# Slots of the second expert mixture inverted by one-hot matmuls, rows fetched per block, first eight blocks fixed

## What is computed

```python
d2 = jnp.sum(xs * xs, axis=-1, keepdims=True) + jnp.sum(centroid * centroid, axis=-1)[None, :] - 2.0 * (xs @ centroid.T)
dist = jnp.sqrt(jnp.maximum(d2, 1e-12))
w, sel = jax.lax.top_k(dist, K)
w = jax.nn.softmax(w.astype(jnp.float32), axis=1).astype(x.dtype)
...
for e in range(E):
    h = jax.nn.silu(xs @ Wg[e] + bg[e]) * (xs @ W1[e] + b1[e])
    out = out + we[:, e:e + 1] * (h @ W2[e] + b2[e])
```

## Time and profile before

| | us |
|---|---|
| median of three runs | 869.1 |
| the three runs | 865.69, 869.1, 869.47 |
| the profiled execution, device time | 866.02 |
| its span, first to last instruction | 864.2 |
| PE busy | 740.8 (86%) |
| DVE busy | 558.0 (65%) |
| ACT busy | 414.8 (48%) |
| POOL busy | 266.5 (31%) |

### The profile page before, as it was taken

The page is one execution under the profiler, slowest core; times in us unless marked ns, Lnnn a source line. Parts: engine busy times, 40 slices in busy tenths (PEclk is TensorE's granted clock), DMA queues, the critical chain, the costliest instruction groups (busy, mean ns, idle before and its releaser), DMA issues.

```text
span 864.2 us, 13607 instructions
## 1 busy us (share of the span) xinstructions
PE 740.8 (86%) x4770; PEld 618.3 (72%) x4770; DVE 558.0 (65%) x1030; ACT 414.8 (48%) x886; POOL 266.5 (31%) x232
## 2 busy tenths in 40 slices
PE   6999999998988399989997998888993089999995
PEld 3688888888954278469974676667662089999994
DVE  3469999998459799276665566776344046556651
ACT  4544444442352189354433565666561046655561
POOL 0174544441006244400025012223213514444442
PEclk9999999999999699879999999998885589999998
DMA  7700000000150000000005665530302559999983
GB/s 242 301 2 18 18 18 18 18 1 1 40 238 0 0 2 2 1 0 1 9 1 141 145 163 132 123 87 2 118 1 67 185 190 282 312 317 314 312 246 65
DMA packets 31249, 89.35 MB, mean 103 GB/s; under 512 B 4310, under 2 KB 22038, under 8 KB 27806
## 3 DMA queue, kind: packets, MB, share of 16 engines
q1 hardware_dynamic: 21805, 42.64, 16.5%
q0 software_dynamic: 9376, 45.84, 16.4%
HBM read 77.25 MB, written 13.85 MB: 105 GB/s over the span
## 4 chain that ended last, share of the span: by engine, by line
PE 54%; DVE 13%; issue 5%; DMA 4%; ACT 4%; POOL 2%; POOLq 0%; SPq 0%; DVEq 0%; ACTq 0%
PE PS L449 50%; POOL token_slots L1544 2%; DMA XB<-token_slots 2%; DVE RW L1721 2%; PE PS L987 1%; DVE SM L2019 1%; DVE WK L1781 1%; PE PS L621 1%; DVE WK L1778 1%; DVE RO L1724 1%; DMA KST<-mask_rows 1%; PE PS L838 1%; PE PS L933 1%; DVE M L2028 1%; PE PS L958 1%
## 5 line engine op out<-in xcount | busy, mean ns | idle before, releaser
L1439 POOL TENSOR_TENSOR PRODL<-RW,PRODH 128x361 fp32r<-128x361 f32 x64 | 64.8, 1015 | 113.1 <-ACT PRODH L1097 109.4
L449 PE MATMUL PS<-CTXH,WKV0H 128*128 128x362 f32 x256 | 86.3, 337 | 9.5 <-DVE RW L1677 8.9
L2019 DVE TENSOR_REDUCE SM<-PS 100x1 f32<-100x362 f32 x128 | 64.8, 531 | 43.9 <-PE PS L449 43.1
L449 PE MATMUL PS<-CTXL,WKV0H 128*128 128x362 f32 x256 | 84.6, 330 | 0.0
L449 PE MATMUL PS<-CTXH,WKV0L 128*128 128x362 f32 x256 | 84.2, 329 | 0.0
L1286 ACT ACTIVATE WK<-PS 120x400 f32<-120x400 f32 (+1 forms) x96 | 48.3, 507 | 43.2 <-PE PS L449 42.3
L449 PEld LDWEIGHTS PS<-CTXH,WKV0H 128*128 128x128 f32 x256 | 48.7, 190 | 15.9 <-DVE RW L1677 11.0
L449 PE MATMUL PS<-KST,QST 97*100 97x362 f32 x128 | 53.7, 431 | 6.4 <-DMA KST<-mask_rows 3.6
L1724 DVE TENSOR_REDUCE RO<-RW 128x100 f32<-128x400 f32 x64 | 56.1, 877 | 2.2
L1097 ACT CAST PRODH<-RW 128x361 fp32r<-128x361 f32 x64 | 31.8, 496 | 53.7 <-DVE RW L1677 53.5
L1561 POOL DMA_INDIRECT out<-YO,TROW x20 | 32.0, 1598 | 79.1 <-DVE YO L2146 75.0
(11 more groups left out here) (302 smaller groups left out, 2068.1 us busy)
## 6 DMA issues: line engine op xcount, KB each, us to landing
KST<-keys_by_head SPq DMA_DIRECT2D x24, 362.0 KB
keys_by_head<-KTHL SPq DMA_DIRECT2D x8, 724.0 KB, 3.4
CTX<-ctxT SPq DMA_DIRECT2D x16, 361.0 KB, 6.6
token_slots<-slots SPq DMA_DIRECT2D x1, 2580.0 KB, 19.5
XB<-token_slots SPq DMA_DIRECT2D x20, 129.0 KB
RW<-WGU SPq DMA_DIRECT2D x1, 2304.0 KB, 8.6
RW<-WKV SPq DMA_DIRECT2D x1, 2048.0 KB, 9.9
RB<-W SPq DMA_DIRECT2D x1, 1368.0 KB
```

What stands on the lines that cost most here:

```text
L449: return pe.matmul(out, lhsT, rhs, start=start, stop=stop)
L1439: pool.tensor_tensor(low, raw, high, ALU.subtract).then_inc(sem["a_products_low_ready"], 1)
L2019: dve.tensor_reduce(SM1[:, q % 2, j:j + 1], PS[0:S, i % 2, 0:KVE], AX_X, ALU.max, negate=True).then_inc(sem["c_maximum_found"], 1)
```

## The change

The scatter of rows goes. In its place the kernel works out, for each slot, which token it holds:

- DVE builds, for each of the 16 groups of 100 pairs, a one-hot matrix of the pair's place in its block (POSITION, 100x128) and one of its block (HOME, 100x20), the latter times the token's number (NAMED) and times its weight in two parts (WEIGHED).
- PE multiplies POSITION by NAMED and sums over the 16 groups. The result holds, at partition p and column k, the number of the token in slot p of block k, plus one. DVE turns it into the row to read (XROW, vacant slots read row 0) and the row to add to (TROW). A second set of 16 products gives the slots' weights (WSLOT).
- The normed tokens are stored once as `token_rows` in DRAM, by SP. POOL fetches the 128 rows of a block by an indirect transfer (`gather_rows`), each after the one before has landed. SP's loads of XB and the copy of `slots` go.
- Block k for k below 8 is expert k's first block; blocks 8 to 19 hold what overflows. So the weight rows of the first eight blocks are known without the router. Their weight loads move ahead: block 0's to SP inside the attention stage, blocks 1 and 2 to POOL before its last batch of that stage, block 3 and down weights 1 right after. The casts of block 0's weights move on ACT to quads 26 and 29 of the attention, the subtractions on DVE to before the output projection's additions. `owners()`, the experts of blocks 8 to 19, moves into block 1.
- The copy of the token rows goes from ACT to DVE. The sum of squares goes from PE (16 of 32 products) to ACT, which squares the rows with an accumulator, 8 operations of 100x256. The square root is taken of the two largest distances only, after the choice. Tables of functions are loaded ahead (`preload_act_table_set`).

The diff, cut to its core (a line "..." marks what is left out):

```diff
@@ -424,21 +442,17 @@
+            load(ROUTE, t["route"], "moe1_small_loaded")
+            load(RAW[0], t["W1"][0:P], "moe1_small_loaded")
             sp.wait_ge(sem["c_turned_scores_summed"], 12 * B)
-            load(RAW[0], t["W1"][0:P], "moe1_small_loaded")
+            sp.wait_ge(sem["moe1_small_loaded"], 48)
+            load(BRAW, t["b1g"], "moe1_small_loaded")
             load(DOWN[0], t["W2"][0:P].rearrange("p (t c) -> p t c", t=6), "moe1_small_loaded")
-            load(ROUTE, t["route"], "moe1_small_loaded")
-            load(BRAW, t["b1g"], "moe1_small_loaded")
-            sp.wait_ge(sem["moe_turned_copied"], 10)
+            sp.wait_ge(sem["rows_copied"], 4)
+            sp.dma_start(XROWS.rearrange("(b s) c -> s b c", s=S), ROWS[:, :, :]).then_inc(sem["rows_stored"], 16)
+            sp.wait_ge(sem["moe_turned_copied"], 6)
...
-            sp.wait_ge(sem["rows_scattered"], 16 * 2 * B)
-            for k in range(NBLK):
-                if k:
-                    sp.wait_ge(sem["tokens_loaded"], 16 * k)
-                if k >= 4:
-                    sp.wait_ge(sem["rows_out_ready"], 2 * (k - 3))
-                load(XB[:, k % 4, :], XSC[k * P:(k + 1) * P], "tokens_loaded")
...
@@ -935,20 +949,24 @@
             for b in range(B):
-                pe.wait_ge(sem["router_squares_ready"], 3 + b // HB)
-                pairs = [(XC[:, k, tok(b)], CENT2[:, k, :]) for k in range(KD)]
-                pairs += [(SQ[:, k, tok(b)], ONES[:, 0:8]) for k in range(KD)]
-                for c, (lhsT, rhs) in enumerate(pairs):
-                    m = mm(PS[0:S, 6, b * 8:(b + 1) * 8], lhsT, rhs, c == 0, c == len(pairs) - 1)
+                for k in range(KD):
+                    m = mm(PS[0:S, 6, b * 8:(b + 1) * 8], XC[:, k, tok(b)], CENT2[:, k, :], k == 0, k == KD - 1)
+            m.then_inc(sem["router_scores_summed"], 1)
+            pe.wait_ge(sem["router_result_ready"], 4)
+            mm(PS[:, 5, 0:B * 8], TRI[:, S:S + P], RTH[:, :], True, True).then_inc(sem["router_scores_summed"], 1)
+            mm(PS[0:S, 7, 0:B * 8], TRI[:, 0:S], RTH[:, :], True, False)
+            for b in range(1, B):
+                m = mm(PS[0:S, 7, 8 * b:B * 8], TRI[:, S:2 * S], RTH[:, 0:8 * (B - b)], False, b == B - 1)
             m.then_inc(sem["router_scores_summed"], 1)
             rows_of(X, 6)
-            chosen = RT[:, 6, :]
-            pe.wait_ge(sem["router_result_ready"], 3)
-            pe.wait_ge(sem["moe1_small_loaded"], 80)
-            mm(PS[0:S, 7, 0:B * 8], EARLIER, chosen, True, False)
-            for b in range(1, B):
-                mm(PS[0:S, 7, 8 * b:B * 8], ONES[0:S, 0:S], chosen[:, 0:8 * (B - b)], False, b == B - 1)
-            mm(PS[:, 5, 0:B * 8], AVG[0:S, :], chosen, True, True).then_inc(sem["router_scores_summed"], 1)
+            for i in range(2 * B):
+                pe.wait_ge(sem["slot_rows_ready"], 2 + i // B)
+                m = mm(PS[:, 7, 64:64 + NBLK], POSITION[:, i, :], NAMED[:, i, :], i == 0, i == 2 * B - 1)
+            m.then_inc(sem["router_scores_summed"], 1)
+            pe.wait_ge(sem["router_result_ready"], 7)
+            for i in range(2 * B):
+                m = mm(PS[:, 7, 96:96 + 2 * NBLK], POSITION[:, i, :], WEIGHED[:, i, :, :], i == 0, i == 2 * B - 1)
...
+                if q in (26, 29):
+                    gu_high(0, (q - 26) // 3)
...
+            act.preload_act_table_set("sqrt_and_others")
+            for i in range(4):
+                act.wait_ge(sem["rows_copied"], i + 1)
+                for x in range(2):
+                    act.activation(SQUARES[:, 2 * i + x, :], ROWS[:, 2 * i + x, :], ACT.Square,
+                                   accum_out=RTC[:, 7, 2 * i + x:2 * i + x + 1]).then_inc(sem["router_squares_ready"], 1)
...
-            copy_rows(ROWS[:, 0, :, :], 2)
             act.wait_ge(sem["moe1_small_loaded"], 80)
             act.wait_ge(sem["zeros_set"], 7)
             act.copy(BROWS[0:40, 0:2 * HID1], BRAW).then_inc(sem["bias_rows_ready"], 1)
-            act.wait_ge(sem["zeros_set"], 8)
-            gu_high(0, 0)
-            gu_high(0, 1)
+            gu_high(1, 0)
             act.wait_ge(sem["router_scores_shifted"], 2)
-            act.activation(RT[:, 0, :], RT[:, 0, :], ACT.Sqrt).then_inc(sem["router_function_taken"], 1)
-            copy_rows(RESID, 6)
+            act.activation(FAR, pairs(TOPS), ACT.Sqrt).then_inc(sem["router_function_taken"], 1)
+            act.preload_act_table_set("exp_and_others")
             act.wait_ge(sem["router_scores_shifted"], 3)
             act.activation(RTC[:, 2, :], RTC[:, 2, :], ACT.Exp).then_inc(sem["router_function_taken"], 1)
+            act.preload_act_table_set("silu_and_others")
+            for i in range(4):
+                act.wait_ge(sem["moe_turned"], 6 + i + 1)
+                act.copy(RESID[:, 2 * i:2 * i + 2, :],
+                         PS[0:S, i, :].rearrange("p (x c) -> p x c", x=2)).then_inc(sem["moe_turned_copied"], 1)
+            gu_high(1, 1)
...
+                if b == B - 2:
+                    pool.wait_ge(sem["router_result_ready"], 3)
+                    pool.wait_ge(sem["c_turned_scores_summed"], 12 * (B - 1))
+                    gather_weights(1)
+                    gather_weights(2)
...
-            pool.wait_ge(sem["slots_cleared"], 16)
-            for c in range(2):
-                pool.wait_ge(sem["router_result_ready"], 4 + c)
-                for b in range(B):
-                    pool.indirect_dma_start(XSC, bass.IndirectOffsetOnAxis(ap=SLOT[:, c, b:b + 1], axis=0),
-                                            ROWS[:, c, b, :], None).then_inc(sem["rows_scattered"], 16)
...
+            def gather_rows(k):
+                if k:
+                    pool.wait_ge(sem["tokens_loaded"], 16 * k)
+                if k >= 4:
+                    pool.wait_ge(sem["moe_turned"], 10 + k - 3)
+                pool.indirect_dma_start(XB[:, k % 4, :], None, XROWS,
+                                        bass.IndirectOffsetOnAxis(ap=XROW[:, k:k + 1],
+                                                                  axis=0)).then_inc(sem["tokens_loaded"], 16)
...
+            pool.wait_ge(sem["expert_weights_low_ready"], N0 + 2)
+            gather_weights(3)
+            gather_down(1)
+            pool.wait_ge(sem["rows_stored"], 16)
+            pool.wait_ge(sem["router_result_ready"], 5)
+            gather_rows(0)
+            gather_rows(1)
             pool.wait_ge(sem["router_result_ready"], 6)
-            gather_weights(1)
             pool.wait_ge(sem["out_stored"], 16)
-            gather_weights(2)
-            gather_down(1)
             for k in range(NBLK + 1):
-                if k + 3 < NBLK:
+                if k + 3 == E1:
+                    pool.wait_ge(sem["router_result_ready"], 9)
+                if k and k + 3 < NBLK:
                     pool.wait_ge(sem["expert_weights_low_ready"], N0 + 2 * k + 2)
                     gather_weights(k + 3)
+                if k + 2 < NBLK:
+                    gather_rows(k + 2)
...
+            gu_low(0, 0)
+            gu_low(0, 1)
...
+            for i in range(4):
+                dve.wait_ge(sem["moe_turned"], 2 + i + 1)
+                dve.tensor_copy(ROWS[:, 2 * i:2 * i + 2, :],
+                                PS[0:S, i, :].rearrange("p (x c) -> p x c", x=2)).then_inc(sem["rows_copied"], 1)
...
+                dve.wait_ge(sem["router_squares_ready"], 10)
+                link(dve.tensor_tensor(v(6), wide(RTC[:, 7, :]), CSQ.unsqueeze(1).to_broadcast([S, B, 8]), ALU.add))
...
+                link(dve.tensor_tensor(v(4), before, over(FIRST), ALU.add))
+                link(dve.scalar_tensor_tensor(v(3), before, float(P), over(OFFSET), ALU.is_ge, ALU.mult))
+                link(dve.tensor_tensor(v(3), v(3), v(4), ALU.add))
+                both = RT[:, 1:3, :].rearrange("p c (b e) -> p c b e", b=B)
+                mine = RT[:, 4:6, :].rearrange("p c (b e) -> p c b e", b=B)
+                link(dve.tensor_tensor(mine, both, v(3).unsqueeze(1).to_broadcast([S, 2, B, E1]), ALU.mult))
+                link(dve.tensor_reduce(SLOTS, mine, AX_X, ALU.add))
+                link(dve.tensor_scalar(OPENS, SLOTS, 0.5 - P / 2, GRID, ALU.add, ALU.add))
+                dve.scalar_tensor_tensor(SLOTS, OPENS, -GRID, SLOTS, ALU.add, ALU.subtract)
+                along = lambda a, n: a.unsqueeze(2).to_broadcast([S, 2 * B, n])
+                link(dve.tensor_tensor(HOME, STARTS[0:S].unsqueeze(1).to_broadcast([S, 2 * B, NBLK]),
+                                       along(pairs(OPENS), NBLK), ALU.is_equal))
+                dve.tensor_tensor(NAMED[:, :, :].rearrange("p (c b) k -> p c b k", c=2),
+                                  HOME.rearrange("p (c b) k -> p c b k", c=2),
+                                  TOKEN.unsqueeze(1).unsqueeze(3).to_broadcast([S, 2, B, NBLK]),
+                                  ALU.mult).then_inc(sem["slot_rows_ready"], 1)
                 for c in range(2):
```

(32 more changed lines are left out.)

223 lines of the change are left out of this document (125 added, 98 removed).

## The result

The changed kernel takes 873.57 us, the median of 20 runs (868.09 to 879.93), against 868.97 for the kernel before, the median of 20 as well. The ratio is 1.0057 with a 95% interval of 1.0037 to 1.0077: **0.6% slower**, where the prediction said 3% faster. The profiled execution took 873.65 us with a span of 871.8, 7.6 us longer than the span in the earlier trace rows. The medians are 4.6 us apart: 3 of the 7.6 are there because the execution in the earlier trace rows was a quick one.

The account below looks back on a forecast made before the run. Taking PE to bound the blocks and a serial POOL queue plus load the hole before them, it summed 26.0 + 1.0 - 0.5 = 26.5 us: 866.0 to 839.5, adjusted toward the median to 841.0 us; range 835.5 to 850.

Parts of the forecast that it names:

- What bounds the kernel: Opening step: PE bounds the blocks at 7.86 us each; the hole before them is POOL's scatters, then a load.
- Part 1: Norm's end to the router's first step: start at 649.2 us against 649.82 before, 0.6 us earlier.
- Part 2: Router's first step to the slot lists: index ready at 661.7 us, second 16 products lying beside the gather.
- Part 3: Fetching the rows: hand-over 0.3 us, landing 3.2, tokens there at 665.2 instead of 691.26, 26.0 us gained.
- Part 4: First blocks: block 1 follows block 0 after 8.0 us, 1.0 us gained; owners' steps lose 0.5.
- Part 5: Edits costed at nothing: weight casts, subtractions and POOL's early gathers in the attention stage, POOL's row-fetch issue in the blocks.
- Rival (b): Blocks: row fetches become a serial loop, block at least landing plus 0.3 us; 888 us at 10.2 landing; chance 0.05.
- (a): Head stays longer through a slower first gather, products, hand-overs, block 0 and owners: 9.0 us lost, 850; chance 0.15 with (c).
- (c): Early weight fetches land late or upset the attention stage; first load costs 5.0 us, casts 2.7: 848.7; counted with (a).
- (d): More gained in head and first blocks, squares included (1.8 us): 3.9 us better, 837.1; chance 0.04.
- the sum: Whole kernel: 26.0 + 1.0 - 0.5 = 26.5 us gained, giving 839.5, or 841.0 us adjusted toward the median.

Follow-up runs that it names:

- all four edits: Changed kernel with rows fetched three blocks ahead and before W1, early weight fetches after the attention stage, DVE's subtractions behind the row copies: 841.51 us, ratio 0.9685.

## Why the prediction was wrong

**What bounds the kernel** was read rightly for the kernel before: with a fetch that comes in time PE sets 7.86 us a block again.

**Part 1** put the router's first step 9.3 us behind the norm's end. It took 6.8 (644.58 to 651.37): the squares follow each other every 0.40 us with their accumulator reads beside them (1.8 us less), and the bias subtraction took 1.57 us, not 2.14. But the norm ended at 644.58, not 639.89, so the step stood at 651.37.

**Part 2** gave 12.5 us to the index; it took 12.2 (651.37 to 663.57). The products behind the second POSITION, the last 8 of 16, were in it with 1.2 us (662.15 to 663.39), as forecast.

**Part 3** gave 3.5 us from the index to the tokens. Fetch 1 follows the landing of fetch 0 and starts at 667.64, which puts that landing near 667.4, 3.8 us after the index: 0.8 for the hand-over (0.3 forecast), 3.1 for the landing (3.2 forecast). PE was still in the slot weights' products until 668.15. Part 2 had these "beside the gather"; they cost about 0.8 us. The net gain up to block 0's turn was 23.1 us of the 26.0.

**Part 4** said 1.0 us gained in the first blocks less 0.5 for the owners: 1.9 gained up to turn 3.

**Part 5 is the step that failed**, in two of its sentences. The first and larger is "In the blocks DVE loses a cast and POOL gains an issue of about 1 us against 3.52 busy of 7.86". It priced the fetch by POOL's busy time. The cost of an operation on an in-order queue that waits is its place: the fetch of block j+4 stands behind the output add of block j, W2 and W1, and has 15.7 us less 6.6 and 4.5 to land, 4.6 us. Block 4's took 8.1. That cost 32.4 us in 16 intervals. Three ahead, or the same two ahead from an earlier place, gave them back; one ahead cost 183 us more. The landing itself was in reach of the prediction: the earlier trace rows has a down gather at 4.9 to 10.2 us, median 6.7.

The second is that POOL's early fetches, "two times 1.3 us", stand before operations "wanted only for the second half of that projection", with DVE's subtractions beside them at no cost. The fetches alone cost nothing (19.8 us from projection to norm); the subtractions stretched whatever POOL had beside them, a product from 1.03 to 3.90 us (21.0) or, together with the fetches, an issue from 0.95 to 4.06. That is 2.4 of the 4.2 us more between projection and norm; the rest is PE at a lower clock, and what lowered it stays open.

**Rival (b)** had the right sign and the right place (PE waiting for rows in the turns), for the wrong reason. It took the block to be the landing plus 0.3 us, deciding the sign from 9.0 on. At 8.1 that gives 8.4 us; the measured 9.88 comes from a cycle over two blocks with the output add in it. Without the serial wait nothing changed. That SP's queue would have kept its turn did not matter either: in a queue of its own the load still took 8.1 us. So its 5% stood mainly for a wait that costs nothing, and a lead that is too short had no rival of its own. Its remark that each fetch stands right behind 1.4 MB of weights did hold, with at least 1.5 us of landing.

**Rivals (a) and (c)** were paid for in part, the 4.2 us of the attention stage, though not through the load or ACT's casts that (c) named. (a) also adds 1.4 us for block 0 where Part 4's own bound, 9.6 against 8.0, gives 1.6. **(d)** had the squares right.

Apart from those two sentences the sum holds: with three blocks ahead and the fetches moved the kernel takes 840.24 us, where 841.0 was forecast for the change as made. That it comes so near is partly luck. In that trace block 0's turn comes 25.9 us earlier than before, of 26.0 forecast, because 2.5 us won ahead of the router and 0.3 behind it make up for 1.9 in the attention stage and 1.1 between index and turn; the first blocks give 2.1 us where 0.5 was the net. That version, at 0.9679 of the kernel before, is the best found; the one with all four edits (0.9685) cannot be told from it.

## What to carry to other kernels

When a load moves from one queue to another, write down what stands ahead of it there, what that waits for, and how many tiles later the load is wanted; the time from the last such wait to the deadline, less the issues in between, must exceed the landing under traffic. An issue slot of 1 us says nothing about it. And DVE operations like these subtractions, long and with both inputs in SBUF, want a place where POOL has nothing urgent, issuing an indirect transfer included.

## What the runs showed of the hardware that I had not expected

**POOL is held up beside a DVE subtraction of two SBUF tiles.** Its product took 3.40 to 3.90 us instead of 1.03, and issues of indirect transfers are stretched just so. In the blocks of the changed kernel, POOL and DVE:

```profile
751.56 0.95 POOL L1575 DMA_INDIRECT XB<-token_rows,XROW  x1 [0.31 <-issue]
...
761.29 2.24 POOL L1575 DMA_INDIRECT XB<-token_rows,XROW  x1 [0.30 <-issue]
...
781.84 2.31 POOL L1575 DMA_INDIRECT XB<-token_rows,XROW  x1 [0.30 <-issue]
```

```profile
752.67 1.58 DVE L2073 TENSOR_TENSOR GUL<-RB,GUH 128x1368 fp32r<-128x1368 f32 x1 [1.19 <-ACT GUH L1348]
...
761.12 1.58 DVE L2073 TENSOR_TENSOR GUL<-RB,GUH 128x1368 fp32r<-128x1368 f32 x1 [1.19 <-ACT GUH L1348]
```

The issue at 751.56 was over before the subtraction at 752.67 and took 0.95 us. The one at 761.29 began just behind the subtraction at 761.12 and ended 0.83 us after it. In the attention stage the issue of 4.06 us ended 1.3 us after the second subtraction. The Trainium skill's "SBUF — State Buffer", section "Who interferes with whom", says that a DVE instruction with two SBUF inputs contends with a GpSimd instruction that reads SBUF, and calls the port pair that they share an exclusive lock. For the product the trace agrees. Of a transfer's descriptors the section infers that such a DVE operation does not stall them. The issues here, which take their row numbers from an SBUF tile, were stretched, so for indirect transfers the measurement decides otherwise. No run here shows a plain transfer issued by POOL in such a place.

**A queue of its own did not make small rows overtake large ones.** 128 KB of 1 KB packets took 8.1 us beside 10 KB packets, in the same queue (block 4's fetch) or in another (the median); issued ahead of the next W1, block 4's landed in under 5.9 us.

**A pause cost more than its length.** In the changed kernel PE's granted clock is 0.50 (1.2 GHz) from 698.82 to 702.82, behind a pause of 3.35 us, and matmuls of 342 columns follow each other at 0.28 us; from 704.82 on it is 1.00 (2.4 GHz) and they follow at 0.16. Behind the next pause, 2.85 us before 720.36, they first follow at 0.16 and from 721.9 on at 0.28. Such stretches make up most of the 9.9 us beside the waits: a mean of 0.95 over the 158 us of the 16 intervals is, by an estimate, 7.9 us lost.
